# Attention steps of a graph network: the mirrored weights ahead of the tails and the preparation

## The reference

```
h = x @ weight;  h_norm = h / max(norm(h), 1e-8)
sim = h_norm @ h_norm.T                       # symmetric
attn = softmax(sim + log(adj + 1e-8), axis=1) # = exp(sim) * (adj + 1e-8), divided by its row sum
x = x + attn @ h + bias
```

## Time and profile before

| what | us |
|---|---|
| median of 3 runs (1344.26 to 1356.36) | 1347.61 |
| the profiled execution | 1345.21 |
| its span from first to last instruction | 1343.4 |
| TensorE busy | 1271.4 (95%) |
| VectorE busy | 1023.0 (76%) |
| ScalarE busy | 627.4 (47%) |
| GpSimd busy | 361.3 (27%) |

### The profile page before, as it was taken

The page is one execution under the profiler, slowest core; times in us unless marked ns, Lnnn a source line. Parts: engine busy times, 40 slices in busy tenths (PEclk is TensorE's granted clock), DMA queues, the critical chain, the costliest instruction groups (busy, mean ns, idle before and its releaser), DMA issues.

```text
span 1343.4 us, 26725 instructions
## 1 busy us (share of the span) xinstructions
PE 1271.4 (95%) x9548; PEld 944.6 (70%) x9548; DVE 1023.0 (76%) x2273; ACT 627.4 (47%) x1480; POOL 361.3 (27%) x422
## 2 busy tenths in 40 slices
PE   4899999989999999989999999999999986899998
PEld 3788888864555555557776776776766665688887
DVE  6998988959355555489989978989889987776642
ACT  3686544716222322266656655756555653311111
POOL 1000000013322232213232322332233222465443
PEclk8999999999999999999999999999999999999999
DMA  9999999720121110134644553534534313350500
GB/s 254 273 340 325 391 365 380 295 99 24 47 63 60 51 63 17 53 98 157 207 148 134 169 176 104 174 126 148 175 115 160 124 66 110 88 149 25 150 25 24
DMA packets 122898, 199.93 MB, mean 149 GB/s; under 512 B 13200, under 2 KB 83856, under 8 KB 122768
## 3 DMA queue, kind: packets, MB, share of 16 engines
q1 hardware_dynamic: 115568, 194.04, 44.7%
q10 hardware_dynamic: 7200, 4.20, 1.1%
HBM read 147.85 MB, written 50.33 MB: 148 GB/s over the span
## 4 chain that ended last, share of the span: by engine, by line
PE 70%; issue 14%; DVE 6%; POOL 6%; DMA 2%; ACT 1%; SPq 1%; ACTq 0%; POOLq 0%; DVEq 0%
PE ps L1817 12%; PE ps L1613 8%; PE ps L1614 8%; PE ps L1575 8%; PE ps L1576 8%; PE ps L1726 7%; PE ps L1711 5%; PE ps L1712 5%; POOL ring L687 4%; PE ps L1778 3%; PE ps L1743 2%; DMA acc<-in_adj 2%; DVE ring L789 1%; POOL small L680 1%; PE ps L1592 1%
## 5 line engine op out<-in xcount | busy, mean ns | idle before, releaser
L687 POOL TENSOR_TENSOR ring<-ring 128x512 f16<-128x512 f32 (+3 forms) x133 | 147.3, 1114 | 343.7 <-ACT ring L1487 343.7
L1575 PE MATMUL ps<-val_hi,ring 128*128 128x257 f16 x1024 | 225.7, 273 | 0.0
L1576 PE MATMUL ps<-val_lo,ring 128*128 128x256 f16 x1024 | 225.7, 273 | 0.0
L1613 PE MATMUL ps<-ring,acc 128*128 128x512 fp8e4 x512 | 195.8, 382 | 3.4 <-DVE acc L926 3.3
L1726 PE MATMUL ps<-hnt 128*128 128x512 f16 (+3 forms) x864 | 196.3, 363 | 1.0 <-DVE ring L1035 1.0
L1614 PE MATMUL ps<-ring,acc 128*128 128x512 fp8e4 x512 | 195.6, 382 | 0.0
L789 DVE STREAM_TRANSPOSE ring<-acc 128x1024 uint8<-128x1024 uint8 x128 | 151.3, 1218 | 23.8 <-DMA acc<-in_adj 23.7
L1711 PE MATMUL ps<-val_hi,ring 128*128 128x257 f16 x490 | 134.9, 275 | 27.7 <-POOL ring L687 27.6
L1711 PE MATMUL ps<-val_hi,hs 128*128 128x257 f16 x534 | 145.8, 273 | 0.9 <-DVE acc L1098 0.6
L1743 PE MATMUL ps<-val_hi,hs 128*128 128x257 f16 x534 | 145.8, 273 | 0.0
L1712 PE MATMUL ps<-val_lo,hs 128*128 128x256 f16 x534 | 145.6, 273 | 0.0
(11 more groups left out here) (234 smaller groups left out, 2396.5 us busy)
## 6 DMA issues: line engine op xcount, KB each, us to landing
acc<-in_adj SPq DMA_DIRECT2D x256, 256.0 KB, 7.8
turned_dram<-ring SPq DMA_DIRECT2D x56, 512.0 KB, 2.9
ring<-turned_dram SPq DMA_DIRECT2D x224, 128.0 KB, 2.8
at_dram<-ring SPq DMA_DIRECT2D x32, 512.0 KB, 9.2
ring<-at_dram SPq DMA_DIRECT2D x64, 256.0 KB, 3.8
ring<-at_dram SPq DMA_DIRECT2D x24, 512.0 KB, 3.9
ring<-at_dram SPq DMA_DIRECT2D x9, 1024.0 KB, 9.6
xs<-in_x SPq DMA_DIRECT2D x12, 256.0 KB, 10.2
```

What stands on the lines that cost most here:

```text
L687: nc.gpsimd.tensor_tensor(lo2[m % 2][:, k:GW], p2t[m % 2][:, k:GW], hi2[m % 2][:, k:GW], ALU.subtract).then_inc(sem["lo2_done"], 1)
L1575: nc.tensor.matmul(ps[:, k % 8, 0:D + 1], lhs, val_hi0[:, t, 0:D + 1], start=(t == 0), stop=False)
L1576: last = nc.tensor.matmul(ps[:, k % 8, 0:D], lhs, val_lo0[:, t, :], start=False, stop=(t == NB - 1))
L1613: nc.tensor.matmul(ps[:, bank + c, :], g_hi[:, t, c * P:(c + 1) * P], src, start=(t == 0), stop=False)
```

## The change

In each attention step the mirrored weights of the next step come ahead of the group tails on VectorE, ScalarE and GpSimd, and on VectorE ahead of the preparation too. The preparation also moves behind the late projection work and the group's sums. No instruction is added, removed or altered.

```
@@ gpsimd, at the end of each step
+                for o in mirrors_at(n + 1):
+                    mirror_low(o)
                 for g, i in tail_at(n):
                     if i == 9:
                         root_var3(g)
-                for o in mirrors_at(n + 1):
-                    mirror_low(o)
@@ vector
-                if n in PREP:
-                    prepare(n)
                 if n in late_at["transposes_n"]:
                     hnt_low(late_at["transposes_n"][n])
...
                 if n + 1 in opens:
                     for b in range(GB):
                         group_sum(order[n][0], b)
-                for g, i in tail_at(n):
-                    group_tail(g, i)
                 if n + 1 < NS:
                     for o in mirrors_at(n + 1):
                         mirror_weights(o)
+                if n in PREP:
+                    prepare(n)
+                for g, i in tail_at(n):
+                    group_tail(g, i)
@@ scalar
-                for g, i in tail_at(n, act=True):
-                    group_tail(g, i)
                 if n + 1 < NS:
                     for o in mirrors_at(n + 1):
                         mirror_high(o)
+                for g, i in tail_at(n, act=True):
+                    group_tail(g, i)
```

## The result

The changed kernel takes **1339.63 us** (median of 10, 1335.33 to 1346.37), the one before 1345.57 beside it (10 runs): ratio **0.9947**, 95% interval 0.9932 to 0.9963, so 5 to 9 us less. The forecast was 1351.0, 3.4 more than the 1347.61 known when it was made. The time lies inside its range, but the sign is wrong.

The account below looks back on a forecast made before the run. TensorE's waits in the attention stage were taken to bound it, with VectorE nearly full there. +0.5 up to 1059 us and +2.9 after, on the profiled 1345.2, gave 1348.6; 2.4 more for the median gave 1351.0, range 1337 to 1358.

Parts of the forecast that it names:

- The waiting GpSimd operation went first: At the port, GpSimd's waiting L687 goes ahead of VectorE's next two-input operation, as read at 816.59 us.
- a tail of 1.2 us is cut: L687 starts amid VectorE's moved tail; its last operation waits 1.0 us, the next L1042 saves 0.30: +0.7 net.
- Term C: A group's tail: VectorE gets up to 1.8 us late, so -0.9 + 1.1 = +0.2 per group; all up to 1059 us +0.5.
- Rival R1: The port hardly matters: GpSimd waits until VectorE's tail is through, or cuts fall between operations; -11.1, 1336.5 us; chance 0.25.
- Term A: Group openings: the mirror's chain comes ahead of VectorE's opening operations; 0.9 us each, five openings until 1059 us, -4.5.
- Term B: ScalarE's tail: L1487 comes 0.93 us earlier, TensorE's waits of 0.97 and 0.35 + 0.16 go; 1.5 per group, if kept.
- What B costs on ScalarE: Moved ScalarE work makes the next L1480 end about 0.5 us later; L1042's net there is nothing, to +0.2.
- Term D: 1059 to 1135 us: cuts of long tails cost VectorE +0.7 to +1.0 each; TensorE +2.9, bounds -6 and +5.
- At no cost: GpSimd's fourth power, SP's reloads and the first group's preparation cost nothing; L1065's wait for loads grows at most 0.7 us.
- What bounds the kernel now: TensorE's attention-stage waits for L687, 33.5 us or 2.5% of the span as ceiling, with VectorE nearly full there.

Follow-up runs that it names:

- The run that forced the forecast's picture: The changed kernel with VectorE waiting for L687's end before the last operation of pieces 11, 13, 14 or 16: 1362.20 us, ratio 1.0126.
- the run of the openings: The kernel before with only VectorE's tail pieces 0 to 10 behind the mirror's products, GpSimd's order as changed: 1341.15 us, ratio 0.9956, loop -6.0.
- the shorter chain: The changed kernel with the second input left out of VectorE's long tail pieces, so their sums and differences are not made: 1326.94 us in one run.
- the kernel with the moved load: The changed kernel with ScalarE's load of a raw quarter (L418) issued four steps later: 1337.92 us, ratio 0.9936, loop -11.0.
- the same order with the load moved: The kernel before with ScalarE's load L418 alone issued four steps later: 1346.43 us, ratio 0.9982, loop -0.5.

## Why the prediction was wrong

**The step that failed** is "The waiting GpSimd operation went first" and what was built on it: "a tail of 1.2 us is cut: its last operation waits 1.0 us". It was read from one place, L1114 behind L1042, and carried over to a chain of L1145 to L1153 that follow each other without a gap. There GpSimd mostly waits until the chain is through: 21 lengthened L687 against 3 held operations of the long pieces. The Trainium skill (SBUF — State Buffer, "SBUF: two separate sides") gives the pair of ports to whichever of the two starts first, for the whole instruction. The rows agree with a lock, but don't say who "starts first" when VectorE's next operation is drawn as started 0.08 us before the last ends; at 851.66 and 847.29 the same order went either way. The run that forced the forecast's picture came out at +13.3; less an estimated 7 for the dearer wait that is +6, near the forecast's +3.4. Group by group it fits too: behind the step of piece 11 that run loses 4.5 at TensorE in each of three groups, less an estimated 4 x 0.33 some 3.2, where Term C has 1.5 + 1.1 = 2.6. So the prices were about right, a little low, and the winner was wrong. Of the 11.8 us between the forecast's +3.4 and the loop's -8.35, 9.2 had arisen by step 123, where the forecast has +0.5 and the kernel is at -8.7. Rival R1 had the mechanism (-11.1; chance 0.25).

**Term A**, -4.5 for five openings: -4.9 measured, and kept, shown alone by the run of the openings. That L1065 would meet L687 there (8 us of held time) was not foreseen and cost TensorE nothing that is seen in these steps.

**Term B**, 1.5 per group: the first part was 0.93 (0.97 forecast). The 0.5 of the next step did not come. TensorE itself is 0.93 early there, so the products had to be 0.93 + 0.51 earlier than before; they are 1.25 (the late L1480 holds up L1042 before them), and L687 waits 0.32 of that for the chain, which leaves just 0.93. With the shorter chain 0.33 came back.

**"What B costs on ScalarE"** was right in the 0.5: at 836.77 L1042 waits 1.43 for L1480, where it waited 0.92 before, and over the stage 16.1 us instead of 12.5. The net of "nothing, to +0.2" looks too low: alone the part is +6.4, with 1.0 per group behind piece 13, and in the changed kernel what it costs eats what B wins.

**Term C**, the ledger of a group's tail, fell with the port: VectorE is 0.5 late near 853 and not 1.8, inside the slack of 0.76 (0.26 is left), so of +1.1 nothing came. Groups 1 to 3 end at -1.9 each, where the forecast had -0.9 + 1.1 = +0.2.

**Term D**, +2.9 for 1059 to 1135: from 1054 to the loop's end it is -0.9 (piece 10) + 1.3 = +0.4; the preparations' steps just ahead of it brought -1.45. Two cuts do stand there (L1161, held 0.97 each time), and two new things. How the +1.3 divides among them is known only for the clock. VectorE's L1159 waits for ScalarE's piece 15, which the change put behind the mirror in the same step, and L1086 behind it:

```profile
1117.38 1.03 DVE L1159 TENSOR_TENSOR hnt<-w_all,hnt 128x512 f16<-128x512 f32 x1 [2.37 <-ACT acc L1506]
```

```profile
1120.82 0.27 PE L1711 MATMUL ps<-val_hi,ring 128*128 128x257 f16 x1 [2.09 <-DVE acc L1086]
```

And TensorE's granted clock fell twice, here in slices of 4 us (clock third from the end); before, it was 1.00 all through this stage:

```profile
1080.00:1084.00 4.00, 4.00 (x26) 3.02 (x24) 3.65 (x14) 2.12 (x5) 1.16 (x1) 0.63 0.00 0
1112.00:1116.00 4.00, 2.61 (x14) 1.90 (x15) 2.63 (x7) 1.18 (x4) 2.26 (x2) 0.71 0.02 4
1116.00:1120.00 4.00, 2.74 (x20) 2.04 (x18) 2.55 (x7) 1.34 (x3) 1.15 (x1) 0.86 0.00 0
```

By slices of 2 us it is at its lower level, 1.2 GHz, from 1079.6 to 1083.0 and from 1113.7 to 1117.1: a matmul of the mirrored block is drawn 0.42 long, not 0.27, and follows in 0.21, not 0.11. Each fall came behind an idle time, of 2.0 us at 1078.80 and of 2.9 at 1113.39, and made the next weighted block 1.66 late. Slack took most of the first; of the second 0.95 was left, judged by the kernel with the moved load, whose clock did not fall. The kernel before idled 2.0 and 3.3 us at the same steps without a fall; the same order with the load moved idled as long and the clock fell both times, at no loss to the loop (-0.5). So the idle time ahead of it did not settle whether a fall comes.

**"At no cost": back loads "at most 0.7"** was mis-sized: the read's wait is 0.4 to 2.8 us in the fourth group, because a load on ScalarE's queue is in flight beside it.

**A reading** under "What bounds the kernel now" was incomplete: before 1059 us TensorE has two more waits over 0.15 us, 0.6 for L1098 and 0.4 for L1042. They are there after the change too, and the sum doesn't use them.

## What to carry to other kernels

A queue's order that puts the chain the bottleneck waits for first is worth what stands ahead of that chain, where the work put behind it has slack; here it paid on VectorE and not on ScalarE, whose moved work delayed the next link, so move each engine's part alone. Where two engines contend for a port, find the contests of the new order one by one: a price read at one place is no guide to who pays it at another. And look beside an unexpected DMA wait for a load on another queue.

## What the runs showed of the hardware

- VectorE's long pieces, back to back, kept a waiting GpSimd operation out for up to 0.92 us (2.08 instead of 1.16), but not always; VectorE, where it loses, waits 1.0 us (L1161 1.26 instead of 0.29). Their one-input forms did so too (1.62).
- Two kernels with the same program up to a place can differ there in who gets the port (L1153 0.41 beside L687 1.49, or 1.38 beside 1.16).
- TensorE's clock went to its lower level for some 3.4 us behind idle times of 2.0 and 2.9 us, and not behind every such time (3.3 in the kernel before): 10 of 15 profiles show such falls in this stage, all from 1000 us on, and 5 none.
- A 512 KB write took 7.4 and 6.8 us beside a 1 MB load on another queue, and 2.6 to 4.6 in the other 54 cases.
